# Moving six fp32r matmul operand buffers off their common alignment in an adaptive-pooling + feed-forward kernel

## What is computed

```python
# conditioning, for each batch
scores  = tanh(x @ W1 + b1) @ v                     # 512 x 128, then 512
mask    = prefix | postfix | cloze, by prompt type  # 512 x 512
p       = softmax(where(mask, scores, -1e30))
pooled  = (p @ x) / count(mask)
# feed-forward, h = layernorm(pooled) * gamma + beta
w1 = (fc1_q - 128) * fc1_scales                     # 512 x 2048
w2 = (fc2_q - 128) * fc2_scales                     # 2048 x 512
y  = silu(h @ w1 + fc1_bias)
z  = y @ w2 + fc2_bias
out = x + pooled + 0.5 * z
```

## Time and profile before

| | |
|---|---|
| median of 3 runs | 1590.62 us (1589.22 to 1591.48) |
| the profiled execution's own time | 1589.56 us |
| its span, first to last instruction | 1587.8 us |
| mean granted TensorE clock | 0.999 |
| instructions | 20995, of which 7259 matmuls |
| DMA | 82.75 MB, mean 52 GB/s |

### The profile page before, as it was taken

The page is one execution under the profiler, slowest core; times in us unless marked ns, Lnnn a source line. Parts: engine busy times, 40 slices in busy tenths (PEclk is TensorE's granted clock), DMA queues, the critical chain, the costliest instruction groups (busy, mean ns, idle before and its releaser), DMA issues.

```text
span 1587.8 us, 20995 instructions
## 1 busy us (share of the span) xinstructions
PE 1572.2 (99%) x7259; PEld 1270.0 (80%) x7259; DVE 952.1 (60%) x1918; ACT 431.8 (27%) x662; POOL 178.1 (11%) x156
## 2 busy tenths in 40 slices
PE   8999999999999999999999999999999999999999
PEld 6778788787887878788787887878878787887887
DVE  7896656655665565646666566556655656456522
ACT  3552222222232222312322223222322223123111
POOL 4101011110101101011110111101111010111100
PEclk9999999999999999999999999999999999999999
DMA  9803022040310404013040220403104040130200
GB/s 282 235 1 80 1 43 65 1 107 1 54 55 13 95 1 87 21 24 83 1 107 1 41 66 1 107 1 54 53 11 97 1 84 23 24 84 0 54 1 27
DMA packets 271311, 82.75 MB, mean 52 GB/s; under 512 B 247498, under 2 KB 248036, under 8 KB 270692
## 3 DMA queue, kind: packets, MB, share of 16 engines
q1 hardware_dynamic: 271152, 81.31, 21.7%
q10 hardware_dynamic: 52, 0.01, 0.0%
HBM read 49.83 MB, written 16.78 MB: 42 GB/s over the span
## 4 chain that ended last, share of the span: by engine, by line
PE 93%; DVE 5%; ACT 1%; issue 1%; DMA 0%; SPq 0%; DVEq 0%; ACTq 0%
PE y_ps L1045 14%; PE z_ps L1079 14%; PE z_ps L1080 14%; PE z_ps L1081 14%; PE y_ps L1046 14%; PE y_ps L1047 14%; PE a_ps L1009 1%; PE a_ps L1014 1%; PE a_ps L1011 1%; PE a_ps L1010 1%; PE a_ps L960 1%; PE a_ps L962 1%; PE a_ps L961 1%; PE a_ps L977 1%; PE a_ps L966 1%
## 5 line engine op out<-in xcount | busy, mean ns | idle before, releaser
L561 ACT ACTIVATE y_f<-y_ps,vec_cols 128x512 f32<-128x512 f32 x256 | 176.6, 690 | 905.5 <-PE y_ps L1047 894.6
L1045 PE MATMUL y_ps<-hT_hi,w_hi 128*128 128x512 f32 x1016 | 406.0, 400 | 0.7 <-DVE w_lo L835 0.6
L1079 PE MATMUL z_ps<-w_hi,y_hi 128*128 128x512 f32 x1024 | 399.2, 390 | 0.0
L1080 PE MATMUL z_ps<-w_lo,y_hi 128*128 128x512 f32 x1024 | 398.4, 389 | 0.0
L1081 PE MATMUL z_ps<-w_hi,y_lo 128*128 128x512 f32 x1024 | 398.4, 389 | 0.0
L1047 PE MATMUL y_ps<-hT_hi,w_lo 128*128 128x512 f32 x1016 | 396.6, 390 | 0.0
L1046 PE MATMUL y_ps<-hT_lo,w_hi 128*128 128x512 f32 x1016 | 396.6, 390 | 0.0
L849 DVE CAST y_hi<-y_f 128x512 fp32r<-128x512 f32 x240 | 109.6, 457 | 246.7 <-PE z_ps L1081 204.0
L1045 PEld LDWEIGHTS y_ps<-hT_hi,w_hi 128*128 128x128 f32 x1016 | 191.0, 188 | 59.3 <-issue 20.3
L1079 PEld LDWEIGHTS z_ps<-w_hi,y_hi 128*128 128x128 f32 x1024 | 192.2, 188 | 41.1 <-DVE y_lo L851 0.8
L1046 PEld LDWEIGHTS y_ps<-hT_lo,w_hi 128*128 128x128 f32 x1016 | 191.2, 188 | 41.9 <-issue 3.4
(11 more groups left out here) (208 smaller groups left out, 1202.7 us busy)
## 6 DMA issues: line engine op xcount, KB each, us to landing
x<-in_x_dram SPq DMA_DIRECT2D x64, 256.0 KB, 3.5
out_dram<-x SPq DMA_DIRECT2D x64, 256.0 KB, 2.2
x_cols<-in_x_dram SPq DMA_DIRECT2D x240, 64.0 KB, 2.2
h_cols<-scratch SPq DMA_DIRECT2D x224, 64.0 KB, 2.1
fc_codes<-in_L_ffn_fc_q_dram SPq DMA_DIRECT2D x8, 1024.0 KB, 15.4
fc_scaled<-in_L_ffn_fc_scales_dram SPq DMA_DIRECT2D x8, 1024.0 KB, 17.3
scratch<-in_L_cond_W_dram SPq DMA_DIRECT2D x1, 256.0 KB, 4.8
b2h<-in_L_ffn_fc_bias_dram SPq DMA_DIRECT2D x1, 256.0 KB, 15.6
```

Of the source, the lines that this page charges most:

```text
L561: nc.scalar.activation(y_f[k % 2][:], y_ps[k % 2][:], ACT.Silu, bias=b1[:, k:k + 1]).then_inc(silu_done, 1)
L1045: mm(o, w1_hi[:, c, cols], hT_hi[:, c, :], start=(c == 0), stop=False)
L1079: mm(z_ps[r][:], y_hi[k % 2][:, rows], w2_hi[:, k, :], start=(k == 0), stop=False)
L1080: mm(z_ps[r][:], y_hi[k % 2][:, rows], w2_lo[:, k, :], start=False, stop=False)
```

## The change

hT_hi, hT_lo, y_hi0 and y_lo0 (the buffers of even k) are allocated 8 words (32 bytes) longer than needed, and the kernel uses them from word 2, 4, 1 and 4 on. The extra words also move all that is allocated behind. Against w1 and w2, whose place stays, hT_hi then starts 8 bytes further on within 512 bytes, hT_lo 48, y_hi0 68, y_hi1 96, y_lo0 112 and y_lo1 128. x, scratch, xs, part, coef, u_rows, e_all and y_f move by 64. m_col becomes column 0 of row_kind in place of a tensor of its own. Shapes, types, instructions, their order and their waits stay.

```diff
-        hT_hi = sb("hT_hi", [P, ND, S], F32R)
-        hT_lo = sb("hT_lo", [P, ND, S], F32R)
+
+        def inset(name, words, cols):
+            return sb(name, [P, cols + 8], F32R)[:, words:words + cols]
+
+        hT_hi = inset("hT_hi", 2, ND * S).rearrange("p (c s) -> p c s", c=ND)
+        hT_lo = inset("hT_lo", 4, ND * S).rearrange("p (c s) -> p c s", c=ND)
...
-        y_hi = [sb(f"y_hi{i}", [P, S], F32R) for i in range(2)]
-        y_lo = [sb(f"y_lo{i}", [P, S], F32R) for i in range(2)]
+        y_hi = [inset("y_hi0", 1, S), sb("y_hi1", [P, S], F32R)]
+        y_lo = [inset("y_lo0", 4, S), sb("y_lo1", [P, S], F32R)]
...
-        m_col = sb("m_col", [P, 1])
+        m_col = row_kind[:, 0:1]
```

## The result

The changed kernel takes 1621.15 us (median of 4 runs, 1620.65 to 1621.59), the kernel before 1590.15 us in the same comparison (1589.22 to 1591.48): a ratio of 1.0196, 95% interval 1.0183 to 1.0208. It is **31.0 us slower**. The forecast of 1566 us was wrong, in its sign too; the rival "the pattern never settles" had given 1619.

The account below looks back on a forecast made before the run. The prediction took TensorE's rate of successive feed-forward matmuls as the bound. From 1589.6 us it took 24.6 us for the matmul operands and nothing else, 1565.0, and with the runs' median 1.1 higher predicted 1566 us, range 1518 to 1605.

Parts of the forecast that it names:

- the pattern never settles: Rival, every fc1 and fc2 step: six changing relations keep steps at 0.2313 us, giving 1619 us; slower case 0.23.
- What bounds the kernel: TensorE's feed-forward matmul steps, 0.2267 us each, 6144 of them, 88% of the span; one nanosecond a step is 6.1 us.
- The reading of the wobble: Steps of 0.22 to 0.24 us behind a stall, then 0.2267: read as weight load and stream getting in each other's way.
- nothing changes: Rival, fc1 and fc2 steps: the surcharge is a fixed price whatever the addresses, giving 1590.6 us; chance 0.27.
- the 13.3 ns: Surcharge of each fc1 and fc2 step over 512 columns at 2.4 GHz (0.2133 us), about 6% of the step.
- The step that failed: fc1 and fc2 operands: a common start was held the worst place, making help twice as likely as harm; faster 0.50.
- The term of the sum: Matmul operands in fc1 and fc2: 4 ns less on each of 6144 steps, -24.6 us.
- The near bound of that choice: Early 256-wide fp32r matmuls showed 11.3 ns surcharge against 13.3, read as a gain of 2 ns a step near at hand.
- The far bound: All fc1 and fc2 steps with a surcharge like plain fp32's: 11.8 ns less a step, -72.5 us.
- The other matmuls: L960 to L962 and L1009 to L1014, some 440: hardly changed, left at nothing.
- VectorE: Writes and reads of y_hi and y_lo, y_hi0 on an odd word: cost 0, covered by 6.7 us of room.
- The range: Whole kernel: 1518 to 1605 us, with the unchanged and mild slower cases, without the wobble for good.

Follow-up runs that it names:

- the trains: The same matmul with its weight load repeated back to back, added at the end of the kernel before in three runs: 1974.14, 1985.97 and 2034.39 us.
- e11_probe3: Kernel before with added repeats of 48 matmuls: 512, 384 and 256 columns at starts equal, 64 and 4 bytes off, fp32r and plain fp32; 2034.39 us.
- e1_all64: Against the kernel before: one 64-byte gap ahead of hT_hi, no insets, so hT and y buffers all lie 64 bytes off w1 and w2; 1621.46 us, ratio 1.0204.
- e12_mixed256: Against the kernel before: 256-byte gaps between hT_hi and hT_lo and between y_hi and y_lo, giving distances 0, 256, 256, 512; 1590.01 us, ratio 0.9997.
- e9_minus16: Against the kernel before: hT 240 bytes off w1 and y 16 bytes off w2, stream minus load -16 in both loops; 1612.68 us, ratio 1.0144.

## Why the prediction was wrong

- *What bounds the kernel* held: the steps of TensorE, 6.1 us for each ns of the step; no other engine, wait or DMA took part, before or after.
- *The reading of the wobble* as a coupling of load and stream held in part: the steps depend on where the stream starts against the load, and the trains show it with all other engines idle. The rival "nothing changes" fell. What did not hold is that the 13.3 ns are such a collision, to be had back: they are the same for 512, 384, 320 and 256 columns at equal starts, and a shorter load doesn't lower them. By the Trainium skill, TensorE: Matmul & The Clock Gate, section Part 2, loading the next tile's weights takes no SBUF read bandwidth from the running matmul. The rival "nothing changes" drew from it that offsets are worth nothing; the runs disagree with that by 31 us for fp32r streams of 512 columns, and leave open whether read bandwidth is the point.
- *The step that failed* is the one from there to the sign: "all operands alike would be the worst place if the two reads collide where they have the same address bits". Starts that are equal, or whole multiples of 256 bytes apart, are the best place for 512 columns: no train beat them, and all of them settled when they stood at multiples of 32 bytes. (Streams 4 bytes short of a multiple of 256 settled too, in the two trains that tried it; with the load 4 bytes on instead, (1,0), it was 232.3 ns.) What I took for the damage, the common start, was what let the pattern settle. The term of the sum was a choice of -4 ns a step; it measured +5.0.
- *The near bound of that choice*, "a gain of 2 ns is near at hand", was misread. It came from five steps of 256 columns with a mean of 118 ns, but those operands start alike, and e11_probe3's train at equal starts also begins at 118 ns and settles at 120.0: the usual 13.3 ns. They were steps not yet settled, and no sign of what another distance gives at 512 columns.
- *The far bound*, 11.8 ns less, was taken from plain fp32, which e11_probe3 shows to be another regime: no offset of fp32r came near it.
- *The rival* "never settles" was right in place, sign and price: 4.6 ns taken from the eight steps behind a stall, 5.04 measured, 1619 us against 1621.15. Its reason was wrong: six different relations aren't needed (e1_all64), and different multiples of 256 do no harm (e12_mixed256). That its price came so near is partly luck: the single distances in the trains cost from 0 to 10 ns. It deserved the largest chance, because the steps of 512 columns that were away from the settled state were slower than it on average.
- *The other matmuls*, costed at nothing, lost 2.9 us: those 541 steps are unsettled too. The projection's streams lie 64 bytes off wc (234.1 ns from one such matmul to the next). The pooling's operands kept distance 0 to each other and still went at 232.8, which points to their neighbours.
- *VectorE* cost nothing, and the odd word hardly lengthened its instructions (429 against 427 ns for the casts into y_hi0, 692 for both kinds of y_lo).
- *The range*, 1518 to 1605, left out the very rival that came true, at 1619.

What stays open is the mechanism inside TensorE: why the surcharge is 13.3 ns at equal starts for each length tried but 448 columns (which repeats 199, 207, 202 and 203 ns, 202.7 in the mean, 16 over), and what has the period of 256 bytes. The runs show the rule for this kernel's shapes, not its cause.

## What to carry to other kernels

Where fp32r matmuls of 512 columns run back to back, keep the stationary and the moving operands at the same place within 256 bytes, and at a multiple of 32 bytes. Padding or a small tensor ahead of one of them that breaks this cost 1 to 2% here without a wait in the profile that showed it. Read the rate from the distances between starts: the good one is 226.7 ns and even, the others have means of 228 to 238 ns and most of them vary from step to step. The mean duration all but hides it (395 against 390 ns here). A stretch of the trace that is away from the steady state tells what leaving it may cost; weigh that before hoping for the opposite, and take it for the same shape, since 256 columns behaved otherwise.

## What was not expected of the hardware

- Starts of load and stream count modulo 256 bytes, and below 32 bytes the common place as well: both at 0, 32, 64 or 256 bytes settle at 226.7 ns, both at 4, 8 or 16 bytes stay at 237.8, 231.1 and 231.0.
- A narrower load doesn't shorten the step: 230 to 232 ns for 96, 64 and 32 columns against 226.7 for 128.
- The same train can go at 226.7 or at 236.7 ns, and within one execution of e9_minus16 some fc2 blocks go at 226.7 and others, at the same starts, at 233.1.
- The direction of a distance counts: a stream that starts 64 bytes further on than the load goes at 228.9 ns, a load that starts 64 bytes further on than the stream at 233.3.
- The disturbance passes from one loop to the next: one stream of three in fc1 off by 64 bytes left only about half of fc2's steps settled. Groups of four pooling matmuls at distance 0 went at 232.8 ns between unsettled ones.
